# Base of the two corner steps of a blocked recurrence: an add on GpSimd in place of identity products on TensorE

## The reference, cut to what matters

```python
kn = k_t / max(norm(k_t), 1e-12)
pred = einsum('bhji,bhj->bhi', S, kn)
r = clip(v_t - pred, -1, 1)
S = a_t[..., None] * S
kp = einsum('bhd,bhde->bhe', kn, S)
S = S + b_t * kn[..., None] * (v_t - kp)[..., None, :]
o = einsum('bhji,bhj->bhi', S, q_t)
R = aR_t[..., None] * R
kpR = einsum('bhd,bhde->bhe', kn, R)
R = R + g_t * kn[..., None] * (r - kpR)[..., None, :]
o = o + einsum('bhji,bhj->bhi', R, q_t)
```

## Time and profile before

| | before |
|---|---|
| median of 3 runs | 3518.9 us (3517.26 to 3531.26) |
| the profiled execution's own time | 3514.6 us |
| its span | 3512.8 us |
| TensorE matmuls busy | 2779.3 us (79%), 49125 instructions |
| TensorE weight loads busy | 1993.9 us (57%), 49147 instructions |
| VectorE busy | 2191.3 us (62%) |
| ScalarE busy | 1443.6 us (41%) |
| GpSimd busy | 549.4 us (16%) |
| mean granted TensorE clock | 0.878 |
| the eight-step chain of `old`, first to last tile | about 1181 us to 2226 us |

### The profile page before, as it was taken

One profiled execution on the slowest core, in us unless ns is written; L12 is line 12 of the kernel. 1 busy time (PEld: TensorE's weight loads), 2 busy tenths in 40 slices (PEclk: granted clock), 3 DMA queues, 4 the chain that ended last, 5 costly groups with the idle time before them and its releaser, 6 DMA issues. The chain is left out here.

```text
span 3512.8 us, 114953 instructions
## 1 busy us (share of the span) xinstructions
PE 2779.3 (79%) x49125; PEld 1993.9 (57%) x49147; DVE 2191.3 (62%) x5703; ACT 1443.6 (41%) x3325; POOL 549.4 (16%) x578
## 2 busy tenths in 40 slices
PE   8977468999956788887888787579998998697744
PEld 5644454444445666666667665356665665375633
DVE  3346325655549978887888786367776555564741
ACT  4343123433342444444444444256665333363410
POOL 0000424555510000000000000000001222062014
PEclk9888778999977899999999999689998998797865
DMA  2100331111110000000000000000001000252013
GB/s 84 57 1 1 109 110 52 40 46 40 34 46 3 4 3 4 4 4 3 4 4 4 4 4 4 2 23 23 24 24 38 0 0 2 92 134 66 5 40 100
DMA packets 69354, 109.08 MB, mean 31 GB/s; under 512 B 10560, under 2 KB 55248, under 8 KB 68080
## 3 DMA queue, kind: packets, MB, share of 16 engines
q1 hardware_dynamic: 57232, 80.34, 7.2%
q0 software_dynamic: 11696, 22.40, 2.5%
HBM read 90.06 MB, written 16.51 MB: 30 GB/s over the span
## 5 line engine op out<-in xcount | busy, mean ns | idle before, releaser
L2872 PE MATMUL psum<-l1d_rw,l1d_cols 64*32 64x32 f32 (+2 forms) x20480 | 244.6, 219 | 102.0 <-issue 73.1
L2872 PEld LDWEIGHTS psum<-l1d_rw,l1d_cols 64*32 64x32 f32 x20480 | 214.0, 109 | 149.3 <-issue 111.5
L2381 POOL TENSOR_TENSOR l2x_qx<-l2x_q,consts 128x128 f32<-128x128 f32 x64 | 25.6, 400 | 1649.9 <-DVE l2x_q L2552 1329.7
L2306 POOL TENSOR_SCALAR l1xs_p<-l1xs_p,l1xs_col 128x257 f32<-128x257 f32 x256 | 238.4, 934 | 242.8 <-DVE l1xs_col L2269 242.2
L2234 ACT ACTIVATE l1xs_p<-psum,l1xs_col 128x257 f32<-128x257 f32 x256 | 122.2, 477 | 256.1 <-DVE l1xs_col L2264 256.0
L2264 DVE TENSOR_REDUCE l1xs_col<-psum 128x1 f32<-128x257 f32 x256 | 107.3, 419 | 138.5 <-PE psum L2186 138.5
L2669 ACT COPY l1d_ya<-psum 128x512 f32<-128x512 f32 x160 | 94.1, 589 | 221.0 <-PE psum L2911 220.2
L3106 DVE TENSOR_TENSOR l1d_rw<-l1d_rw,l1d_tots 128x512 f32<-128x512 f32 x240 | 152.9, 686 | 48.0 <-PE psum L2872 46.8
L2186 PE MATMUL psum<-l1xs_keys,l1xs_qx 128*32 128x257 f32 x2048 | 160.8, 393 | 4.3 <-ACT l1xs_p L2234 4.3
L2198 PE MATMUL psum<-l1xs_pt,l1xs_vals 32*128 32x512 f32 x1152 | 162.0, 637 | 1.3 <-DVE l1xs_pt L2276 1.3
L2811 PE MATMUL psum<-l1d_src,l1d_wp 128*128 128x128 f32 x1024 | 138.6, 292 | 26.3 <-ACT l1d_src L2674 24.7
(11 more groups left out here) (567 smaller groups left out, 6919.0 us busy)
## 6 DMA issues: line engine op xcount, KB each, us to landing
l2f_w<-in_l2f_w SPq DMA_DIRECT2D x16, 768.0 KB
l1xs_vals<-in_ctx_strips SPq DMA_DIRECT2D x16, 576.0 KB, 3.7
l0x_ctxT<-in_ctxT SPq DMA_DIRECT2D x16, 516.0 KB, 3.5
l1xs_keys<-in_ctxT SPq DMA_DIRECT2D x16, 516.0 KB, 3.3
l2x_ctxT<-in_ctxT SPq DMA_DIRECT2D x64, 129.0 KB, 2.1
l1d_wp<-in_l1d_wp SPq DMA_DIRECT2D x1, 2048.0 KB, 7.8
l2f_acc<-l2f_zero SPq DMA_DIRECT2D x8, 256.0 KB, 4.3
l2f_sums<-l2f_acc SPq DMA_DIRECT2D x8, 256.0 KB, 4.9
```

What stands on the lines that cost most here:

```text
L2306: nc.gpsimd.tensor_scalar(p[:, t % 4, :S2], p[:, t % 4, :S2], col[:, 2, t % 4:t % 4 + 1], None, ALU.mult).then_inc(s["norm"], 1)
L2872: mm = nc.tensor.matmul(k.ps[bank0 + pr + e // per * 2][b * T:b * T + T, e % per * w:(e % per + 1) * w], cols[rr, n, e * 128 + b * T:e * 1 ...
```

## The change

The two corner steps z and z2 are issued without a base, so each loses its two identity products, and each small product starts its own group. ScalarE copies the bare halves to `ya` as before, but signals two new semaphores, `bare` and `bare2`. GpSimd gets a program of its own: for each tile and each half it waits for ScalarE's copy, adds the base (v for z, `rd` for z2) to `ya` in place, and signals `t` or `t2`, which `step_u` and `step_wr` wait for as before. The step p keeps its identity products.

```diff
-             "norm", "turn", "steps")
+             "norm", "turn", "steps", "bare", "bare2")
@@
-                    take(i - 2, "z_mm", ya, "B", "t")
+                    take(i - 2, "z_mm", ya, "B", "bare")
@@
-                    take(i - 2, "z2_mm", ya, "B", "t2")
+                    take(i - 2, "z2_mm", ya, "B", "bare2")
@@ step_z
-                apply(i, "B", wide(3), ya, "z_mm", v)
+                apply(i, "B", wide(3), ya, "z_mm")
@@ step_z2
-                apply(i, "B", wide(4), ya, "z2_mm", rd)
+                apply(i, "B", wide(4), ya, "z2_mm")
@@
+        @block.gpsimd
+        def _(pool):
+            def add_base(i, bare, base, done):
+
+                for j in range(2):
+                    half = slice(j * 512, (j + 1) * 512)
+                    pool.wait_ge(s[bare], i * 2 + j + 1)
+                    nc.gpsimd.tensor_tensor(ya[:, half], ya[:, half], base[:, half], ALU.add).then_inc(s[done], 1)
+
+            for i in range(NT):
+                add_base(i, "bare", v, "t")
+                add_base(i, "bare2", rd, "t2")
```

## The result

| | before | after |
|---|---|---|
| median (20 runs each, the same chips) | 3522.7 us (3508.7 to 3539.8) | 3536.2 us (3518.4 to 3556.4) |
| ratio | | 1.0041, 95% interval 1.0026 to 1.0056 |
| the profiled execution | 3514.6 us, span 3512.8 | 3535.8 us, span 3534.1 |

The changed kernel is slower by 0.41%, some 14 us; the forecast was 18 us faster, and 3536 lies above the range. The loss is inside the 0.5% that the prediction called no change. The two profiled executions differ by 21 us, more than the medians, so times in what follows are taken from the timed runs, and the profiles show where things happen.

The account below looks back on a forecast made before the run. Neither PE nor VectorE alone bounds the kernel; PE's late 256-instruction blocks and VectorE's `clip` limit the gain. 12 + 16 - 1.4 + 1.6 - 10 = 18 us less, from the median 3518.9 to 3501 us; range 3474 to 3527.

Parts of the forecast that it names:

- the 0.5% that the prediction called no change: Whole kernel: a measurement can tell about 0.5%, 17.6 us, from no change.
- removal: 12 + 16 + 1.6, and 7.6 in the last passes: Identity products gone beside fills: z gains 12 us, z2 16, fewer instructions 1.6; last two passes save 1.91 us a step.
- the wait: 1.4, and 7.4 in the last passes: Copy-then-add chain before wr takes 1.4 us of z2's 16; each last-pass step gains 1.86 us of wait.
- VectorE's loss to the adds: `advance` beside z: 0 to 2.5 us a tile, taken as 1.25, costing 10 us over fourteen tiles.
- Fetching leaves 30 of 53.5 us: PE's late 256-instruction blocks in fourteen tiles with fills: z keeps 14 us, z2 16; the rest returns as stops.
- `clip` would then release y2: VectorE before y2: `clip` caps z's gain, 14 to 12 us, and releases y2 in more than two of twelve tiles.
- Beside z2 the loss is covered: VectorE idles 3.18 us before its next work beside z2, so a loss to the adds there is covered.
- the rival of the turns: VectorE and GpSimd take turns at `advance` beside z and z2: sum +20 us, 3539; chance 0.18.
- The new wait: ScalarE's copy then GpSimd's add: `t` at 2.5 to 2.6 us after the step instead of 0.7; hidden after z.
- PE's stops at whole blocks and their growth: PE stops after whole multiples of 256 instructions; issue stops on L2872 and L2911 grow by about a third.
- u not released by GpSimd beside the fills: Sign at PE's waits: GpSimd releases wr in most tiles, u hardly ever.
- the pace of a tile: Sign in the stretch of tiles: pace goes from 71.3 to about 70 us.

Follow-up runs that it names:

- z alone: Against the kernel before, only z's base is moved to GpSimd adds; z2 keeps its identity products and ScalarE's copy: 1.0035.
- the exchange of the two pieces: Changed kernel with VectorE's `keep_s` of level 1 put before `advance_s` of level 1: 1.0017; the same exchange in the kernel before, as control: 1.0007.
- z2 alone: Against the kernel before, only z2's base is moved to GpSimd adds; z keeps its identity products: 0.9988.
- memsets: Changed kernel with each GpSimd add replaced by a scratch memset of about the same length that reads nothing, base left out: 1.0005.
- the runs on the last passes: Changed kernel with the last two tiles keeping identity products: 1.0044; only those two changed: 1.0010; changed kernel with filler products in those two: 1.0054.

## Why the prediction was wrong

Three terms of the sum were off, and a fourth was not in it. To compare them with the runs, the last two passes have to be counted in, where the prediction set 4 x 1.91 us of products against 4 x 1.86 us of wait. The times are those of the runs with both steps; the last two have wide intervals, taken from two ratios each.

| | forecast | measured |
|---|---|---|
| removal: 12 + 16 + 1.6, and 7.6 in the last passes | 37 us | 17 us (10 to 23) |
| the wait: 1.4, and 7.4 in the last passes | 9 us | 18 us (9 to 28) |
| VectorE's loss to the adds | 10 us | 13 us (4 to 21) |

Of the 32 us between the forecast and the result, 20 lie in the removal. It alone is clearly outside its noise.

**"Fetching leaves 30 of 53.5 us": the term that failed most.** For z it held: 12 us beside the fills and 4 in the last passes forecast, 13 measured (7 to 19). For z2 it did not: 14 to 16 beside the fills and 4 in the last passes, against 5 (interval -2 to 12). Both removed are 17 us, and z's and z2's ratios multiply to 0.9949, so the measurements agree among themselves. I took a block that ends earlier to bring the next one earlier by as much. The thirteen-tile means say that this fails after z2: 1.6 us gained, 1.1 to 1.7 given back before the next fill. In the trace of z2's removal 0.8 us a tile of it is stops for issue, and 0.65 is work at a lower granted clock. Why the next block comes no earlier stays open.

**The clock: put at nothing without a reason.** The prediction has no term for it. With both products removed, the program is at the lower level for 25 us more, and in the changed kernel for 55. At somewhat over half a microsecond each, the estimate above, that is some 14 us of the 20 that the removal lacks, and some 15 of what the wait costs once the products are gone. These prices are argued from one stretch; that the time at the lower clock grows is shown.

**What VectorE loses to the adds: the argument failed, the size less so.** I bounded it by 0 and 2.5 us a tile and took 1.25, 10 us in all, "since half of what VectorE does beside z reads PSUM". Beside z it is 1.9 us a tile in the trace of z alone, between my value and the bound; with z2's adds it is 2.7. In time it is 13 us with both steps (1.0041 less 1.0005) and 20 us with z alone (1.0035 less 0.9978), under the 26 that I had for the bound. The argument looked at the wrong moment. `keep_s` of level 1 comes after `advance_s` in VectorE's order, and a z that ends 1.9 us earlier puts both adds beside `advance` alone: adds from 1695.51, multiplications from 1695.33. The change moved its own adds into the worst place, and the exchange of the two pieces agrees with that. That `clip` would then release y2, and its margin be what is eaten, was right: eight of twelve tiles.

**Beside z2 the loss is covered, as said.** z2 alone is 0.9988, and its removal 0.9986; the two differ by less than their noise of some 10 us. So the rival of the turns had its mechanism right and its place half right: it put 18 of its us beside z2, where no loss shows. That its 3539 us lie near the measured 3536 is luck: it took the removal at its forecast value, 28 us, and set 48 us of losses against it.

The Trainium skill, SBUF — State Buffer, section Who interferes with whom, states that a VectorE instruction with two SBUF inputs contends with a GpSimd instruction that reads SBUF, not with one that only writes it, and calls the shared ports an exclusive lock. This case's runs agree on each point: 824 ns under adds, 687 under memsets, 772 where more of the adds lie beside reads of PSUM, and almost no overlap of the two.

**The new wait.** Beside the fills it costs little, as forecast: PE waited for GpSimd 5.8 us between 1250 and 2120, in six of twelve tiles. In the last passes I had 2.55 us a step. Three of the four waits are 2.3; one is longer, two adds beside VectorE's last inversion:

```profile
2194.19 3.33 POOL L3061 TENSOR_TENSOR l1d_ya<-l1d_ya,l1d_rd 128x512 f32<-128x512 f32 x2 [13.80 <-ACT l1d_ya L2669]
...
2197.58 2.72 PE L2911 MATMUL psum<-l1d_ya,l1d_wideX 64*64 64x64 f32 x46 [3.15 <-POOL l1d_ya L3061]
```

Together they are 7.4 us longer than ScalarE's were, against 7.6 us of products saved: nothing, as forecast, and the runs on the last passes allow a loss of 0 to 9 us. Even so the memsets cost 0.52% once both products are removed, some 18 us (1.0005 less 0.9953), and 0.15% with z alone, 5 us. 8 us of the 18 are the last passes; the rest would fit the 28 us more at the lower clock, which is argued and not shown.

**What held:** PE's stops at whole blocks and their growth (71 to 91 us in two rows, near the third forecast), u not released by GpSimd beside the fills, 64 adds, an unhindered add of 1.25 us. **What did not:** wr was released by GpSimd in half of the tiles and not in most, the pace of a tile went to 71.9 us and not to 70, and L2906 has 64 matmuls left, not 128, since z and z2 had 64 each of the 192. The sum as measured: -0.47% removal, +0.52% wait, +0.36% reads, which is +0.41%; it has to come out, since each part is the difference of two neighbouring kernels.

## What to carry to other kernels

Before work is moved to GpSimd, find what VectorE does at the moment at which it will run, in the new timing and not the old, and count an operation with two SBUF inputs there as standing still for the add's length; what the engine's idle time before its next consumer does not cover is lost (here, with both steps, 13 us of the 38 by which VectorE's multiplications grew). The runs favour placing such adds beside masked copies or reads out of PSUM. Giving the sum to the engine that reads PSUM anyway is the other way, which here was not shown to be faster than before. Where TensorE stops for its instructions, long products that take few instructions are partly free cover, and removing them can also bring more time at the lower clock: measure what their bare removal brings before paying for a replacement.

## What the runs showed that I had not expected

- The exclusion is nearly complete and goes both ways: 4.1 us for 1.9 us of multiplications and 2.5 us of adds; a memset of 1.38 us in the same place leaves VectorE at 687 ns. VectorE's masked copies out of PSUM do not stop: 21 of 384 columns that lay beside the adds of the changed kernel have a median of 570 ns, the 63 others 563.
- It hits small operations as hard as large ones. In the last passes four multiplications of 64 columns took 2.96 us under two adds; four such take 0.8 us elsewhere in the same kernel:

```profile
1706.77 0.80 DVE L3229 TENSOR_TENSOR l1d_tmp<-l1d_lt,l1d_xi 128x64 f32<-128x64 f32 x4
...
2177.74 2.96 DVE L3229 TENSOR_TENSOR l1d_tmp<-l1d_lt,l1d_xi 128x64 f32<-128x64 f32 x4
2177.87 2.52 POOL L3061 TENSOR_TENSOR l1d_ya<-l1d_ya,l1d_v 128x512 f32<-128x512 f32 x2 [22.79 <-ACT l1d_ya L2669]
```

- Of TensorE's 93 stops for issue between 1256 and 2112 us, up to 2.6 us long, 82 lie whole multiples of 256 of its recorded instructions apart (within 16, since some records are missing); the 11 others all stand before L2927, where the values are projected. A removed product can come back in part as such a stop in the next stretch.
- Products taken away from TensorE came with a lower granted clock (0.870 against 0.874 over the whole program, by the timed runs), so part of what was saved was spent again on slower work.
- The same kernel's profiled thirteen tiles differed by 9 us between two executions; a single profile of each of two kernels can't rank parts of this size. The account of the last passes, built on one, did not survive its timed runs.
